# Adding the two squared halves of the channels on VectorE ahead of one product with ones, in a fused decoder layer

## The reference

```python
x = x + attn(layernorm(x), Wq, Wk, Wv, Wo)     # 16 heads of 16, weights (q k)^2 under a causal mask, normalised
x = x + align(ctx, layernorm(x))               # dynamic time warping of 77 context rows onto 1024 rows
x = x + ffn(layernorm(x), ...)                 # butterfly up to 1024, GELU, butterfly down to 256
```

```python
def _pairwise_euclidean(a, b):                 # a: 77 context rows, b: 1024 normalised rows, 256 channels
    aa = jnp.sum(a * a, axis=-1)[:, None]
    bb = jnp.sum(b * b, axis=-1)[None, :]
    ab = a @ b.T
    return jnp.sqrt(jnp.maximum(aa + bb - 2.0 * ab, 0.0))
```

## Time and profile before

| | |
|---|---|
| time, median of 3 runs | 974.54 us (970.09, 974.54, 976.97) |
| the profiled execution's own time | 971.9 us |
| its span, first to last instruction | 970.1 us |
| mean granted TensorE clock | 0.899 of full speed |
| PE busy (matmuls) | 781.5 us, 81% of the span |
| DVE busy | 565.8 us, 58% |
| ACT busy | 430.3 us, 44% |
| POOL busy | 124.7 us, 13% |

### The profile page before, as it was taken

One profiled execution on the slowest core, in us unless ns is written; L12 is line 12 of the kernel. 1 busy time (PEld: TensorE's weight loads), 2 busy tenths in 40 slices (PEclk: granted clock), 3 DMA queues, 4 the chain that ended last, 5 costly groups with the idle time before them and its releaser, 6 DMA issues.

```text
span 970.1 us, 12570 instructions
## 1 busy us (share of the span) xinstructions
PE 781.5 (81%) x3919; PEld 380.3 (39%) x3919; DVE 565.8 (58%) x2539; ACT 430.3 (44%) x644; POOL 124.7 (13%) x306
## 2 busy tenths in 40 slices
PE   4679899699779698986969878769799641499998
PEld 2244223343223262222343213335484541356657
DVE  5614456332455522698989998738889888413002
ACT  0146986267667347773537757324303100033130
POOL 2113131112302111221112211100000000000000
PEclk9889999799979889996979889879899866599999
DMA  9793331935520764260491550310010011100001
GB/s 299 178 146 49 49 37 66 161 34 76 88 25 1 133 127 57 32 75 10 103 159 15 74 74 13 42 18 14 5 32 26 12 34 33 29 1 11 32 1 43
DMA packets 52132, 58.55 MB, mean 60 GB/s; under 512 B 22631, under 2 KB 31819, under 8 KB 52067
## 3 DMA queue, kind: packets, MB, share of 16 engines
q1 hardware_dynamic: 50979, 53.57, 32.0%
q0 software_dynamic: 1088, 4.19, 1.3%
HBM read 36.24 MB, written 21.50 MB: 60 GB/s over the span
## 4 chain that ended last, share of the span: by engine, by line
PE 45%; DVE 31%; DMA 8%; ACT 7%; issue 5%; SPq 3%; DVEq 0%; POOL 0%; POOLq 0%; ACTq 0%
PE psS L976 8%; PE psO L993 7%; PE psS L1121 7%; PE psW L1131 6%; DVE FOLD L774 5%; DVE FOLD L753 5%; DMA ARENA<-qk_parts 4%; ACT ARENA L612 3%; DVE FOLD L772 3%; PE psW L1038 3%; DVE FOLD L751 2%; PE psW L1051 2%; PE psW L1031 2%; SPq L414 2%; PE psW L1059 2%
## 5 line engine op out<-in xcount | busy, mean ns | idle before, releaser
L612 ACT ACTIVATE ARENA<-psS 128x1024 f32<-128x1024 f32 (+3 forms) x384 | 296.1, 810 | 148.9 <-PE psS L976 145.7
L976 PE MATMUL psS<-ARENA 96*128 96x512 bf16 (+3 forms) x768 | 191.4, 345 | 61.2 <-DMA ARENA<-qk_parts 38.0
L993 PE MATMUL psO<-ARENA 128*32 128x512 f32 (+3 forms) x1536 | 171.8, 521 | 5.1 <-DVE ARENA L708 4.7
L567 POOL TENSOR_SCALAR_AFFINE_SELECT ARENA<-ARENA 128x256 f32<-128x256 f32 x256 | 109.8, 433 | 451.0 <-ACT ARENA L612 448.0
L976 PEld LDWEIGHTS psS<-ARENA 96*128 96x128 bf16 x768 | 54.7, 100 | 241.9 <-ACT ARENA L612 137.7
L1131 PE MATMUL psW<-W2E,ARENA 128*128 128x256 f32 x512 | 114.3, 384 | 20.6 <-DVE ARENA L956 20.6
L1131 PEld LDWEIGHTS psW<-W2E,ARENA 128*128 128x128 f32 x512 | 98.1, 192 | 36.7 <-DVE ARENA L956 21.4
L675 ACT ACTIVATE ARENA<-psS,BEFF 128x512 f32<-128x512 f32 x64 | 43.6, 687 | 123.5 <-PE psS L1121 123.5
L1022 PE MATMUL psW<-IDENT,XX 128*128 128x128 f32 x192 | 34.3, 328 | 45.7 <-DVE XX L838 38.4
L1031 PE MATMUL psW<-XX,ARENA 128*128 128x512 f32 x128 | 64.0, 636 | 7.4 <-DVE XX L846 2.9
L868 DVE TENSOR_TENSOR X<-X,psW 128x512 f32<-128x512 f32 x32 | 21.7, 679 | 80.9 <-PE psW L1111 49.8
(11 more groups left out here) (116 smaller groups left out, 807.9 us busy)
## 6 DMA issues: line engine op xcount, KB each, us to landing
ARENA<-qk_parts SPq DMA_DIRECT2D x192, 128.0 KB, 7.0
qk_parts<-ARENA SPq DMA_DIRECT2D x16, 768.0 KB, 6.6
out<-ARENA SPq DMA_DIRECT2D x16, 256.0 KB, 2.2
X<-in_x POOLq DMA_DIRECT2D x3, 1024.0 KB, 9.4
dist<-ARENA SPq DMA_DIRECT2D x4, 425.0 KB, 10.5
MORE<-dist SPq DMA_DIRECT2D x32, 52.6 KB
path<-MORE SPq DMA_DIRECT2D x52, 32.4 KB
dist<-ARENA SPq DMA_DIRECT2D x4, 300.5 KB
```

The lines of the kernel that those rows point to most:

```text
L567: pool.affine_select(out=blk, in_=blk, compare_op=ALU.is_ge, fill=0.0, base=0, pattern=[[0, 2], [1, P]], channel_multiplier=-1).then_inc(s ...
L612: nc.scalar.activation(A[:, (2 * G + a) % A_PAIRS, :, 0:N], psS[:, a, :, 0:N], ACT.Square).then_inc(s_sq, 1)
L976: ins = nc.tensor.matmul(psS[:, a, j, 0:N], KST[0:STACK, g % 2, 2 * a + j, kt * P:(kt + 1) * P], QST[0:STACK, g % 2, 2 * a + j, q0:q0 + N] ...
L993: ins = nc.tensor.matmul(psO[32 * j:32 * j + 32, o % 2, q0 - qc * HALF:q0 - qc * HALF + N], V1[:, kt, GH * g + j], A[:, (2 * G + j // 2) % ...
```

## The change

The pair of half-channel squares is added on VectorE, and the product with ones is made once per half of the rows. DVE gets a part in the odd `turn_s` units (i = 2h + 1): it waits for ACT's evictions of both turn_s units of that half, adds SQT[:, 1] into SQT[:, 0] in place (128 partitions x 512 float32), and counts a new semaphore. PE makes the two products with the context as before, waits for that semaphore, and makes one product with ones where two were.

```diff
+        s_squares = sem("s_squares")
...
+                elif kind == "turn_s" and u[2] % 2:
+                    _, b, i = u
+                    cols = slice(i // 2 * HALF, (i // 2 + 1) * HALF)
+                    for j in (i - 1, i):
+                        dve.wait_ge(s_free[bank("turn_s", b, j)], made("turn_s", b, j))
+                    SQT = BACK[b][1]
+                    nc.vector.tensor_tensor(out=SQT[:, 0, cols], in0=SQT[:, 0, cols], in1=SQT[:, 1, cols], op=ALU.add).then_inc(s_squares, 1)
                 elif kind == "products":
...
                     for k in range(KD):
                         nc.tensor.matmul(W[0:S], CTXT[:, b, k], SNT[:, k, cols], start=k == 0, stop=False)
-                    for k in range(KD):
-                        ins = nc.tensor.matmul(W[0:S], ONES[:], SQT[:, k, cols], start=False, stop=k == KD - 1)
+                    pe.wait_ge(s_squares, 2 * b + h + 1)
+                    ins = nc.tensor.matmul(W[0:S], ONES[:], SQT[:, 0, cols], start=False, stop=True)
```

## The result

| | before | changed |
|---|---|---|
| median of 11 runs each | 973.03 us (970.09 to 976.97) | 978.6 us (976.82 to 980.98) |
| ratio, 95% interval | | 1.0058 (1.0042 to 1.0075) |
| the profiled execution's span | 970.1 us | 975.0 us |
| mean granted TensorE clock | 0.899 | 0.893 |
| PE busy / DVE busy | 781.5 / 565.8 us | 780.3 / 570.8 us |

The changed kernel is slower by 0.58%, 5.6 us. Ratios and the microseconds worked out from them are those on record; they are not quotients of the two medians and differ from them by up to 0.12%. The traced execution of e5 was a disturbed one (1090 us), so no figure is taken from it. The forecast was +3.0 us, at 977.5, with 967 to 984.5 as its range.

A forecast was written before the change was run, and what follows sets the result against it. No single bound: the chain is 45% PE, 31% DVE. -3.4 (batches 0 and 1) + 7.55 (batch 2) - 1.7 (batch 3) + 0.6 (clock) = +3.0 us on 974.5, so 977.5 us; range 967 to 984.5.

The forecast's parts named there:

- batch 2 decides, by DVE's place in the list: Batch 2's dist units: DVE reaches the additions late, behind backward steps, so PE waits; not hidden, +7.55 us.
- The two waits: Batch 2, dist 0 and dist 1: PE waits mid-group for DVE's addition, 6.3 us and then a further 3.0 us.
- +7.55: Batch 2: PE reaches the scores behind dist 1 at 607.8 instead of 600.23, hanging only on DVE's arrival.
- 0.6 for the clock: Batch 2: half clock for a few us after the first wait, and perhaps after the second, adds 0.6 us.
- the others are hidden: Batches 0, 1 and 3: six additions of 0.70 us hide under 1.72 us of context products; 5.2 us less on PE.
- a shorter second wait may bring another short spell: Batch 2, dist 1: the second wait may bring another short half-clock spell; part of the 0.6 us added.
- the third rival: From 607 to the end of attention the clock stays down after dist 1: 5.8 us more, 983.3 us; chance 0.08.
- in batch 3 1.7 us: Batch 3, behind warp 0: the removed products with ones return 1.7 us.
- All eight are hidden, 967.6: First rival: DVE abreast of PE in batch 2, so all 6.9 us of products come off, 967.6 us; chance 0.14.
- from there to the end of attention PE and ACT lead: From 577.96, batch 2's first transposes, PE and ACT lead; DVE nearly full, 32.3 of 38 us, PE 33.8.

The follow-up runs named there:

- e5: The changed kernel with batch 2's two additions moved in DVE's list, behind normal 3 and backward 17; 970.62 us, ratio 0.996 to the kernel before.
- e6: The changed kernel with the additions on GpSimd in place of DVE, at the same places of the list; 970.94 us, ratio 0.9969 to the kernel before.
- e9: e5 with batch 3 as before the change, both products and no addition; 970.56 us, ratio 0.9965 to the kernel before.
- e10: e5 plus two extra products with ones, result unused, just ahead of batch 3's second dist unit; 970.92 us, ratio 0.9961 to the kernel before.
- e4: Kernel before with one product with ones per half, no addition, no wait; half the squares left out, layer not computed; 968.44 us, ratio 0.9943.
- e12: e6 plus two extra products with ones in PE's idle time of batch 3; 969.43 us, ratio 0.9946 to the kernel before.

## Why the prediction was right, and where its sizes were off

**Right: batch 2 decides, by DVE's place in the list.** The two waits came with the releaser named, in the middle of the group, and nowhere else. The first was put at 6.3 us and was 5.73; the second at 3.0 and was 1.64. The end of the stretch, said to hang on DVE's arrival alone, was put at +7.55 with 0.6 for the clock, 8.15; it was 21.64 - 14.42 = +7.22. DVE came to the first addition 6.91 us after PE's first context product (590.09 - 583.18), where 7.27 was counted (593.08 - 585.81): 0.36 less, part of it because a scan's row overlaps the next start. The additions took 0.66 to 0.69 against 0.70.

**Right: the others are hidden.** Six times DVE waited for ACT, and PE did not wait for the addition. Batch 0 gave 11.09 - 9.38 = 1.71 us for 1.72; batch 1 gave 1.47, as its second unit runs in part at the lower clock in both kernels (4.91 us before, 4.30 changed).

**Right as to the sign of the clock, wrong as to its place.** After the first wait the clock was 0.50 from 590 to 594 and returned before the second wait. PE's time in hand took all of the cost: PE still waited 1.64 us at the second addition, so the stretch ended by DVE's arrival alone, and the 0.6 us that was added for the clock was not paid. Part of the second wait's 1.64 for 3.0 is this: the slower clock used up time that PE would otherwise have waited. The step "a shorter second wait may bring another short spell" did not come: 1.00 over 600 to 604, and the third rival (the clock stays down after dist 1) with it. The rule of the Trainium skill, "TensorE: Matmul & The Clock Gate", section "HAM oscillation — how this bites in real kernels", agrees with the trace behind the first wait (0.50 over 590 to 594) and not behind the second (1.00 over 600 to 604); the second came out shorter, at 1.64 us, than the waits of that section's example, so it is a weak test of the rule.

**The step that failed: "in batch 3 1.7 us".** It was 12.64 - 12.49 = 0.15. The prediction took the removed passes at full-clock worth and did not ask what the clock does behind the shortened unit. The traces put the missing time there: the first dist unit gave 0.67 us (5.49 before, 4.82 changed), and the second, run partly at the lower clock, took back 0.51 (3.47 to 3.98; up to 0.84 in other versions).

**The sum redone.** From the stretches of the two traces: -1.71 (batch 0) - 1.47 (batch 1) + 7.22 (batch 2) - 0.15 (batch 3) = +3.9 us. Forecast for the same: +3.0. So two errors, -0.93 in batch 2 (0.6 of it the clock term) and +1.57 in batch 3, partly cancelled, and 0.25 lies in batch 1; that the sum of the stretches came within 1 us of the forecast is in part luck. The measured 5.6 us (4.1 to 7.3) in the first series and 4.3 (2.5 to 6.1) in the second stand a little above 3.9. What the first series has beyond it is in no stretch that the change touches: the stretches between, with the same code, differ by up to 4 us from trace to trace. Whether the change moves them, by shifting the phase of clock and DMAs, stays open.

**A rival priced too low.** "All eight are hidden, 967.6" priced batch 2's products at their full 1.72 us. e6, e9 and e10 took PE's waits away, and C2-C3 did not shorten; even e4, with no addition, shortened it by only 1.08. The reading "from there to the end of attention PE and ACT lead" was true, but DVE was just behind; the prediction used that only for the loss and not for the gain.

## What to carry to other kernels

When every engine walks one common list, an operation given to another engine is not done where the list has it but when that engine gets there: read in its order of time how far behind or ahead it is, and put the operation at its own place for that moment, or on the engine that walks beside the producer, after a look at what its work does to others: here each addition on GpSimd held DVE for about 1 us. Before counting an engine's saving in a stretch, look which engine would be waited for next: here DVE was 1 us behind PE. And work taken from a tensor engine that already idles in short pieces can be given back in clock: here 1.72 us less of passes in batch 3 made its stretch 0.15 us shorter.

## What was not expected of the hardware

A dist unit with two passes of ones less took 3.97 to 4.31 us where the full one took 3.46, in six traces of seven, by the granted clock falling to half ahead of or within its context products (0.67 over 644 to 648 in the changed kernel). Two products whose result nobody reads, put in ahead of it, brought it to 2.57 us with the clock at 1.00 (e12; in e10 the clock might have held without them), and moved its start by 0.7 us. With no addition at all (e4) it was 2.60 without them: there the earlier slow stretch ended sooner, with the ones of the first unit at 1.02 us, so whether the second fall comes depends on more than the amount of work, and this was not taken apart further.

GpSimd adds 128x512 float32 from SBUF in 1.27 us, DVE in 0.66 to 0.69. While GpSimd did so in the warp, an instruction that DVE began just after it did not end before it: 1.29 and 1.14 us for scans of 0.286 (e6), 1.53 for 0.46 and 1.09 for 0.17 (e12).
